# GpSimd waits for the landing of an earlier gather in front of every second tile's gathers

## What is computed

```python
x = x + L0(group_norm(x))                 # frequency filters, 1x1 convolutions, a mask
x = x + L1(group_norm(x))                 # below

proj   = einsum('bchw,oc->bohw', x, Wc) + bc          # 1x1 convolution, 256 -> 256
flows  = einsum('bchw,koc->kbohw', x, Woff) + boff    # 4 heads, an offset (x, y) per pixel
weights = softmax(einsum('bchw,kc->bkhw', x, Wwt) + bwt, axis=1)
feats  = grid_sample_bilinear_zeros(proj, base + flows[k])   # 4 heads, 4 corners each
out    = einsum('kbohw,bkhw->bohw', feats, weights)
```

## Time and profile before

| | us |
|---|---|
| median of 3 runs | 712.74 |
| lowest and highest | 708.37 and 716.56 |
| the profiled execution, whole | 709.86 |
| its span, first to last instruction | 708.1 |
| outside the span | 1.8 |
| gathers, first and last start in the span | 246.1 and 683.2 |

### The profile page before, as it was taken

How to read it: one execution, slowest core, us unless ns; L and a number is a source line. 1 busy time by engine, 2 the same in 40 slices (tenths; PEclk the granted TensorE clock), 3 DMA queues, 4 the chain that set the end, 5 groups by cost and what they waited for, 6 DMA issues and landing times.

```text
span 708.1 us, 10473 instructions
## 1 busy us (share of the span) xinstructions
PE 605.9 (86%) x2889; PEld 479.4 (68%) x2889; DVE 549.0 (78%) x1316; ACT 362.1 (51%) x892; POOL 364.0 (51%) x385
## 2 busy tenths in 40 slices
PE   1999799999997888598959977997889889699787
PEld 0444475778886777486848866886777767587666
DVE  6999774579998775696849766985698759698567
ACT  0298885788995442352543536363544535355221
POOL 0030593235554475466556656666565665666630
PEclk9999999999999566699879989998989979989899
DMA  9900001137767799799989999999999999999992
GB/s 358 373 23 0 0 1 47 44 89 214 213 212 238 238 370 334 283 357 401 350 326 340 400 359 367 367 371 351 393 358 360 385 383 326 381 379 357 375 347 60
DMA packets 77366, 197.04 MB, mean 278 GB/s; under 512 B 7337, under 2 KB 36812, under 8 KB 77196
## 3 DMA queue, kind: packets, MB, share of 16 engines
q0 software_dynamic: 43488, 154.55, 59.2%
q1 hardware_dynamic: 33836, 42.03, 17.0%
HBM read 168.05 MB, written 28.51 MB: 278 GB/s over the span
## 4 chain that ended last, share of the span: by engine, by line
DVE 32%; another core or an unknown queue 14%; issue 13%; PE 7%; POOL 0%; DVEq 0%; ACT 0%
DVE ps L1166 20%; PE ps L1536 3%; DVE ps L1163 2%; DVE xs L1180 2%; PE ps L1486 2%; DVE wq L1166 1%; DVE wvs L1166 1%; DVE wvs L1173 1%; PE ps L1562 1%; DVE wq L1173 1%; PE ps L1563 0%; DVE weights L1116 0%; PE ps L1595 0%; DVE pos L1079 0%
## 5 line engine op out<-in xcount | busy, mean ns | idle before, releaser
L956 POOL DMA_INDIRECT v<-table,index x252 | 236.2, 937 | 152.8 <-issue 64.0
L1536 PE MATMUL ps<-v 128*128 128x256 f32 x786 | 215.7, 422 | 49.5 <-issue 24.0
L1536 PEld LDWEIGHTS ps<-v 128*128 128x128 f32 x786 | 163.5, 213 | 87.1 <-issue 38.9
L1166 DVE SCALAR_TENSOR_TENSOR ps<-v,weights,ps 128x256 f32<-128x256 f32 x489 | 214.5, 482 | 3.4 <-DVE ps L1166 1.5
L1313 ACT ACTIVATE v<-ident,weights 128x128 f32<-128x128 f32 x464 | 139.3, 388 | 13.9 <-remote 11.2
L1326 ACT COPY pick_mask<-ps 128x512 f32<-128x512 f32 x18 | 10.5, 585 | 137.5 <-remote 115.6
L1405 PE MATMUL ps<-wq,s_ring 128*128 128x256 f32 x288 | 68.1, 380 | 1.0 <-ACT ps L1249 0.9
L943 POOL TENSOR_TENSOR xs<-xs,v 128x512 f32<-128x512 f32 x36 | 45.1, 1274 | 46.0 <-DVE v L1013 46.0
L1326 ACT COPY sample<-ps 128x512 f32<-128x512 f32 x17 | 9.9, 584 | 104.3 <-remote 57.5
L1180 DVE TENSOR_TENSOR xs<-ps,xs 128x512 f32<-128x512 f32 x35 | 23.9, 682 | 46.9 <-remote 46.9
L1405 PEld LDWEIGHTS ps<-wq,s_ring 128*128 128x128 f32 x288 | 53.9, 191 | 9.4 <-issue 2.9
(11 more groups left out here) (174 smaller groups left out, 955.2 us busy)
## 6 DMA issues: line engine op xcount, KB each, us to landing
table<-stage SPq DMA_DIRECT2D x72, 256.0 KB, 3.2
xs<-in_x_dram SPq DMA_DIRECT2D x11, 768.0 KB, 11.1
out_dram<-xs SPq DMA_DIRECT2D x28, 256.0 KB
v<-table,index POOLq DMA_INDIRECT x252
early<-const_syn POOLq DMA_DIRECT2D x18, 192.0 KB, 3.8
ana<-const_ana SPq DMA_DIRECT2D x1, 2304.0 KB, 20.0
out_dram<-xs SPq DMA_DIRECT2D x7, 238.0 KB
stage<-table,index POOLq DMA_INDIRECT x36
```

Source lines behind the costliest of these rows:

```text
L956: nc.gpsimd.indirect_dma_start(places[a], None, table, bass.IndirectOffsetOnAxis(ap=index[:, t, k:k + 1], axis=0)) \
L1166: V.scalar_tensor_tensor(to, corner, weight, ps[:, DVE_SUM, i * C:(i + 1) * C], ALU.mult, ALU.add).then_inc(added, 1)
L1536: m = T.matmul(ps[:, PE_SUM[i], 0:C], diag[2 * u + i][n], places[a][:, q * C:(q + 1) * C], start=n == 0, stop=n == len(mine) - 1)
```

## The change

GpSimd gets one more wait in front of the first gather of every even tile from tile 2 on. It waits until the second gather (head 1) of the tile before has landed. GpSimd has by then issued all four gathers of that tile, so that the third and fourth can still be under way when it goes on. All else is as before.

```diff
                         for t in range(NT):
                             if t in FIRST:
                                 pool.wait_ge(index_ready, GROUP_OF[t] + 1)
+                            if t >= 2 and t % 2 == 0:
+                                pool.wait_ge(landed[place_of(t - 1, 1)], 16 * use_of(t - 1))
                             for k in range(HEADS):
                                 a = place_of(t, k)
                                 if t >= RING:
```

## The result

The change makes the kernel slower: 757.42 us (754.2 to 759.27, four runs) against 712.35 us (now four runs as well), a ratio of 1.065 with a 95% interval from 1.060 to 1.070. All ratios here leave out runs in a slower state that single executions fall into, so they can differ a little from the quotient of the medians. The prediction was 716 us, with a range from 698 to 730. The profiled execution took 759.27 us whole, 757.5 us in its span.

The account below looks back on a forecast made before the run. The consumers' loop of PE and DVE was taken to bound the kernel, DMA close behind. 709.86 us + 4 for longer pairs - 1 for avoided pauses gave 713; with 2.9 to the median, 716 us, range 698 to 730.

Parts of the forecast that it names:

- the ring's waits: POOL's waits when all 16 gather places are taken, 96.8 us; claimed to dissolve into the new wait.
- L: Time from a gather's start on POOL to its landing; taken as 5.8 us for the awaited gather.
- the release: POOL going on after the awaited gather has landed, put at about 0.1 us a pair.
- A run of eight that follows a pause lies between the first and the second: Choice of 5.8 us from start to landing, between 4.6 after a pause and 6.5 after a run of ten.
- The sum's +4 us: Cost over the pairs of tiles: 12.3 us a pair against 12.18, 35 x 0.12.
- Each delay of POOL shortens that queue: Argument that start to landing contains the queue in front, so waiting shortens it; spoke against a slower pair.
- the slower rival: The wait bites at even tiles: 12.5 us or more a pair, +11 to +22 us; chance 0.32.
- The margin at the restart: When POOL goes on, two gathers hold 2.85 us of DMA work, restart takes 1.5; 0.2 us lost a pair.
- The consumers' loop sets the pace, with gathers in reserve: PE and DVE use a pair, POOL refills: 12.18 us a pair, DMA engines with next to nothing to spare.
- The landed reserve of ten microseconds: Gathers land ten microseconds before DVE reads them; the slower case would eat this in some thirty pairs.
- The pause helps TensorE: POOL's pause lets PE's releases through, shrinking DVE's 94.4 us of waits: -13 us, bound -38; chance 0.28.
- It does nothing: The awaited gather has nearly always landed when POOL comes to the wait; time stays 712.7 us; chance 0.05.

Follow-up runs that it names:

- under1: The change with its wait for the third gather of the tile before, so one gather stays under way; 790.9 us, 1.121 of the kernel before.
- half_after_b: The changed kernel with gathers of 2 KB a descriptor, the lower two corners left out; 658.59 us, 0.984 of the kernel before.
- under3: The change with its wait for the first gather of the tile before, so three stay under way; 704.69 us, 0.996 of the kernel before.
- rolling4_b: In place of the change's wait, every gather from tile 1 on waits for the same head's gather of the tile before; 726.6 us, 1.089 of the kernel before.
- after_3: The changed kernel, unchanged, run again in the fourth session; 754.3 us, 1.135 of the kernel before.
- before_3: The kernel before, unchanged, run again in the fourth session; 665.64 us.
- after_again: The changed kernel, unchanged, run again in the third session; 755.33 us, 1.062 of the kernel before.
- half_before_2: The kernel before with half gathers, the lower two of four corners not fetched, in the fourth session; 625.92 us, 0.939 of the kernel before.

## Why the prediction was wrong

*The way of the change through the kernel was right.* The new wait binds in every pair, the ring's waits dissolve into it, and a pair takes five issues, L and the release. under1 and half_after_b came out as the formula said beforehand; under3 and rolling4_b missed what was expected of them and fit it with the L that their own traces show.

*The step that failed is the size of L.* I took 5.8 us, between 4.6 and 6.5, and 0.1 us for the release, 5.9 together; together they were 7.3. "A run of eight that follows a pause lies between the first and the second" was read from the earlier trace rows, where I asked when the DMA engines ran empty. But the wait counts 16 increments for a gather, so the last of them decides, and the engines' mean share in a window of 1 us says little of when that one comes (argued from the kernel's count; no run took it apart). Also, those last gathers had nothing behind them, while the awaited one has two gathers in the same queues; that this delays it is argued too. The prediction's upper end of 6.5 would have given 12.8 us; the truth was beyond both ends. The sum's +4 us should have been 35 x 1.35 = +47.

*"Each delay of POOL shortens that queue" failed too.* It was my reason against the slower rival. The median landing time fell, to 6.5 us in after_3, from 15.8 where the queue was deep, but the awaited gather hasn't gained by it: it still takes 7.3 us to the restart. One reason can be seen: behind each restart the bytes come slowly for some microseconds (119 and 262 GB/s in the windows above, 106 in the one below).

*The margin at the restart was mispriced.* I counted two gathers, 2.85 us, less 1.5 us for the restart, and so 0.2 us lost. That margin holds at most for the DMA engine that is furthest behind; the others are ahead by then, which is again argued, but its effect is seen. In after_3 the engines have drained at the moment POOL goes on (518.69), and over 390 GB/s are reached only in the last of these windows:

```profile
518.00:519.00 1.00, 1.00 (x6) 0.90 (x5) 1.00 (x4) 0.00 (x0) 0.31 (x1) 1.00 0.65 262
519.00:520.00 1.00, 1.00 (x6) 0.87 (x6) 1.00 (x4) 0.00 (x0) 0.69 (x2) 1.00 0.07 29
520.00:521.00 1.00, 1.00 (x7) 0.87 (x6) 1.00 (x3) 0.00 (x0) 0.87 (x1) 1.00 0.70 106
521.00:522.00 1.00, 1.00 (x6) 0.90 (x5) 0.70 (x2) 0.00 (x0) 0.82 (x1) 1.00 0.79 307
...
524.00:525.00 1.00, 0.36 (x2) 0.00 (x0) 0.86 (x5) 1.00 (x3) 0.69 (x2) 1.00 0.83 220
...
526.00:527.00 1.00, 0.70 (x2) 0.30 (x2) 1.00 (x4) 1.00 (x5) 0.85 (x1) 1.00 1.07 395
```

The restart itself takes the 1.5 us that I read from the trace. But it isn't covered, and the slow microseconds behind it were not in the sum at all.

*What bounds the kernel.* "The consumers' loop sets the pace, with gathers in reserve" is right at most for the execution that I had. Where the kernel before takes 666 us it is the DMA engines with a deep queue. The landed reserve of ten microseconds was real at the end of that execution, but a reserve only delays a loss: with the change DVE waits up to 3.3 us for landings by 330 us, in the first six pairs.

*The rivals.* The slower one had the right mechanism, decision point (12.4 us a pair) and sign, with 0.32, and its signs in the profile came (DVE and PE wait for landings, DMA share below 0.95); at its upper price of +22 us it was half of what came. "The pause helps TensorE" was half seen: DVE's waits for TensorE fell by half with the change and to 83 us in under3, but under3 isn't faster, so nothing hung on them. "It does nothing" fell far off. The rule of the Trainium skill ("DMA: Bandwidth & Descriptors", "Anatomy of one DMA — SWDGE (gpsimd) path": about 2.0 us plus bytes over 436 GB/s) led there, with its estimate of 3.2 us for 512 KB. The trace comes near its rate (413 GB/s in the best slices of before_3), but a gather in a stream takes longer to land: 6.2 to 15.8 us in the median.

*Still open* is why the kernel before has two speeds. In the profiles of the slower one (first and third session, and the execution shown above) DVE waits long for "remote" releases of TensorE; in the faster one these waits are missing and the queue is deep. TensorE itself is idle in the slower one for nothing that the profile shows ("issue"). This is line 1536 in the window from 320 to 620 us, in the kernel before as shown ahead:

```profile
PE ps L1536 <- issue: 15.3, 23, 1.7
```

In the same window before_3 has:

```profile
PE ps L1536 <- issue: 0.2, 1, 0.2
```

The granted clock of TensorE over the span is 0.913 in the one and 0.969 in the other. No run shows which of these is cause and which is effect. The change's profiles show such waits in the first measurement and in after_again, and not in after_3, at the same time, so they are no part of its loss. Whether they come from the chip, which was another in each session, or from something in the kernel's course wasn't settled: half_before_2, meant for this, fell into a session of the faster kind.

## What to carry to other kernels

Before you add a wait for a transfer that is still under way, write down the chain it closes: issues in front of it, its start to landing under load, the release. Compare that with the period that the loop has now. What stays under way must cover the restart, and the mean over the engines is too kind a measure of that: beside a kernel before of 710 us, two gathers of 512 KB didn't cover it, three were at the edge, four did. Beside one of 666 us only two were tried, and there three may not be enough: four issues and the 7.0 us of under3 make 12.0 us, where a pair takes 10.84 (an estimate; no run shows it). And a queue that feeds a saturated resource wants depth: rolling4_b, with four under way at any time, was 8.9% slower than the kernel before in the faster kind of session, which has 11 or 12 (before_3).

## What the runs showed of the hardware

- The rate of the gathers goes with the depth of their queue, even while the DMA engines count as busy: 407 GB/s at a share of 1.03 with 11 or 12 gathers queued (before_3), 343 to 349 at 0.95 to 0.96 with four (rolling4_b), 321 to 325 at 0.91 to 0.92 where the queue drains once in eight gathers (the change). The kernel before at 710 us, whose depth its profile doesn't give, has 365 and 368 at 0.98 and 0.99.
- From POOL's start of a gather on a drained queue to the first bytes it takes 1.3 to 1.6 us (293.15 in the kernel before, 518.69 in after_3). In after_3 the next six microseconds had between 106 and 356 GB/s, and 395 came behind them.
- The same program took 710 us in two sessions and 666 to 669 us in two others, with a spread of under 1% within each session of the faster kind. A comparison across sessions would have been off by 6%.
